# Forty extra full-height products in the first head of an attention kernel

## The reference

```
xn = layernorm(x)
q, k, v = split(xn @ w_qkv.T)          # 16 heads of 16
q, k = rope(q), rope(k)
attn = softmax(q @ k.T / 4)
x + (attn @ v) @ w_out.T + (silu(xn @ wg.T) * (xn @ wu.T)) @ wd.T
```

## Time and profile before

| | before |
|---|---|
| median of 3 runs | 2939.09 us (2939.03 to 2942.41) |
| the profiled execution | 2940.6 us |
| its span | 2938.8 us |
| mean granted PE clock | 0.989 |
| busy share of PE, DVE, ACT | 98%, 91%, 84% |

### The profile page before, as it was taken

How to read it: one execution, slowest core, us unless ns; L and a number is a source line. 1 busy time by engine, 2 the same in 40 slices (tenths; PEclk the granted TensorE clock), 3 DMA queues, 4 the chain that set the end, 5 groups by cost and what they waited for, 6 DMA issues and landing times.

```text
span 2938.8 us, 67492 instructions
## 1 busy us (share of the span) xinstructions
PE 2871.5 (98%) x27448; PEld 1062.6 (36%) x27448; DVE 2671.8 (91%) x2938; ACT 2478.5 (84%) x4635; POOL 523.0 (18%) x1086
## 2 busy tenths in 40 slices
PE   6999998999999999999999999999999999999999
PEld 4656664233333333333333333333333333333336
DVE  7667667999999999999999999999999999999952
ACT  4544554999999999999999999999999999999972
POOL 4666673000000000000000000000000000000000
PEclk9999997999999999999999999999999999999999
DMA  3233331011111111111111111111111111111125
GB/s 116 89 92 116 100 94 54 25 32 31 31 31 31 31 31 31 31 31 31 31 31 31 31 31 31 31 31 31 31 31 31 31 31 31 31 31 31 31 64 179
DMA packets 124601, 137.14 MB, mean 47 GB/s; under 512 B 43264, under 2 KB 103296, under 8 KB 124288
## 3 DMA queue, kind: packets, MB, share of 16 engines
q1 hardware_dynamic: 124288, 132.79, 16.6%
HBM read 88.15 MB, written 34.08 MB: 42 GB/s over the span
## 4 chain that ended last, share of the span: by engine, by line
PE 88%; ACT 5%; DVE 4%; issue 2%; DMA 1%; POOL 0%; SPq 0%; DVEq 0%; ACTq 0%; POOLq 0%
PE psum L749 37%; PE psum L714 21%; PE psum L785 17%; PE psum L623 5%; PE psum L594 4%; ACT probs L948 3%; PE psum L696 2%; ACT acc_sb L918 1%; DVE row_max L1355 1%; PE psum L638 1%; ACT hT L842 1%; DVE stats L1114 1%; DVE xnT L1138 1%; DVE h L1271 0%; ACT silu L855 0%
## 5 line engine op out<-in xcount | busy, mean ns | idle before, releaser
L1355 DVE TENSOR_REDUCE row_max<-psum 128x1 f32<-128x1024 f32 x2022 | 2303.0, 1211 | 27.8 <-PE psum L714 27.0
L948 ACT ACTIVATE probs<-psum 128x512 f32<-128x512 f32 x4096 | 2179.1, 595 | 164.3 <-PE psum L785 61.9
L749 PE MATMUL psum<-probs,v_op 128*32 128x256 f32 x15872 | 1297.3, 399 | 0.0
L785 PE MATMUL psum<-q_op,k_op 51*128 51x512 f16 x4096 | 854.9, 381 | 19.1 <-ACT probs L948 15.6
L714 PE MATMUL psum<-k_op,q_op 48*128 48x512 f16 x4070 | 808.2, 389 | 7.2 <-DVE row_max L1355 4.7
L714 PEld LDWEIGHTS psum<-k_op,q_op 48*128 48x128 f16 x4070 | 196.7, 93 | 855.3 <-DVE row_max L1355 537.1
L749 PEld LDWEIGHTS psum<-probs,v_op 128*32 128x32 f32 x15872 | 312.5, 108 | 524.2 <-issue 485.5
L785 PEld LDWEIGHTS psum<-q_op,k_op 51*128 51x128 f16 x4096 | 365.0, 94 | 257.4 <-ACT probs L948 68.0
L1095 POOL TENSOR_TENSOR acc_sb<-acc_sb,inv_rows 128x512 f32<-128x512 f32 x64 | 81.7, 1276 | 1686.7 <-DMA inv_rows<-inv_dram 1686.7
L623 PE MATMUL psum<-xnT,wf 128*128 128x512 f16 x768 | 179.0, 379 | 0.6 <-DVE v_space L1261 0.6
L849 ACT ACTIVATE parts<-qk_rot 128x512 f16<-128x512 f32 x64 | 40.1, 627 | 149.1 <-POOL qk_rot L1018 149.1
(11 more groups left out here) (115 smaller groups left out, 1104.1 us busy)
## 6 DMA issues: line engine op xcount, KB each, us to landing
qk_dram<-staged SPq DMA_DIRECT2D x64, 256.0 KB, 4.9
q_op<-qk_dram SPq DMA_DIRECT2D x128, 128.0 KB
k_op<-qk_dram SPq DMA_DIRECT2D x128, 128.0 KB
x_ln<-in_x SPq DMA_DIRECT2D x16, 512.0 KB, 4.4
x_res<-in_x SPq DMA_DIRECT2D x16, 512.0 KB, 5.3
y_dram<-y_blk SPq DMA_DIRECT2D x16, 512.0 KB, 3.3
k_op<-qk_dram SPq DMA_DIRECT2D x128, 64.0 KB
q_op<-qk_dram SPq DMA_DIRECT2D x128, 64.0 KB
```

The costliest lines, as they stand in the source:

```text
L749: mm = pe.matmul(bank(7)[32 * j:32 * j + 32, n0:n1], v_op[:, h % 2, t, :], probs[:, g3 % PROBS, j * BANK + n0:j * BANK + n1], start=(t == ...
L785: pe.matmul(bank(b), k_op[r:e, h % SLOTS, t * P:(t + 1) * P], q_op[r:e, h % SLOTS, j * BANK:(j + 1) * BANK], start=True, stop=True).then_i ...
L948: nc.scalar.activation(probs[:, g2 % PROBS, j * BANK:(j + 1) * BANK], bank(b), ACT.Exp, scale=to_score).then_inc(s2_used, 1)
L1355: nc.vector.tensor_reduce(row_max[:, hl % 2, t, half:half + 1], psum[:, 2 * half * BANK:(2 * half + 2) * BANK], AX.X, ALU.max).then_inc(s1 ...
```

## The change

After each `max_half` of the steps 0 to 19 PE makes one more product: the 16-bit identity (128 x 128) times 512 columns of all 128 rows of `k_op`, into bank 7. That is 40 products. Nothing reads them, and no semaphore is added or counted. Bank 7 is first needed by `weigh_v` in step 21, which overwrites it.

```diff
+        def keep_busy(c):
+
+
+            if c < FIRST2 + PV_LAG - 1:
+                pe.matmul(bank(7), identh[:, :], k_op[:, 0, 0:BANK], start=True, stop=True)
+
         def step(c):
...
             if c < N1:
                 max_half(c, 0)
+            keep_busy(c)
...
                     weigh_v(0)
                     if c < N1:
                         max_half(c, 1)
+                    keep_busy(c)
```

## The result

| | before | after |
|---|---|---|
| median of 4 runs each | 2939.61 us | 2962.97 us (2961.35 to 2963.67) |
| span of the profiled execution | 2938.8 us | 2960.7 us |
| mean granted PE clock | 0.989 | 0.986 |

The ratio of the times is 1.0081, with a 95% interval of 1.0069 to 1.0093. The forecast was 2961.4 us.

What follows compares the result with a forecast made beforehand. PE, DVE and POOL set the pace in turn within 48 us at half clock, PE in (b). Lost cover and new products 15.8 us plus switches 6.5 us gave 22.3 us on 2939.1: 2961.4 us, range 2940 to 2966.

Steps and rivals of the forecast that it cites:

- (b): Stretch from 479.8 to 503 us, 13 steps (2 to 14) at 1.2 GHz, paced by PE at 1.71 us each.
- The step of seven products: In (b), a step holds seven products one after another, 2.99 us for 1.71; 15.8 us over the stretch.
- The switch: Going between half-height and full-height products on PE loses 0.11 to 0.16 us each time, 0.13 taken.
- The term of 6.5 us: Price of 50 switches between half-height and full-height products on the path, at 0.13 us; bounds 0 and 8 us.
- The clock would not be held: Around stage B, the new products would not keep PE at full clock; forecast with clock as before, chance 0.70.
- The case that the clock never falls: Rival: full clock from `k_neg` through (b), 2934.2 to 2940.4 us; chance 0.18, including a clock back equally early.
- the 2.1 us at the products with v: DVE's waits of 0.58, 0.75 and 0.75 us for PE at the first products with v, saved if the clock is full.
- The eight products of the steps 15 to 18 and those of step 19: After (b): the eight hidden under DVE's 1.15 us; step 19 costs 0 to 0.9 us, taken as 0.
- The cover of 0.04 us: In steps 15 to 18, the time to spare for the new products under DVE's 1.15 us.
- the clock back within (b): Rival: full clock returns during the stretch, +10.8 us or 2949.9 us; chance 0.12.
- the slow 48 us: Half-rate clock from just before 475 us to 522.7 us; anything the change gives back or adds lies there.
- A lost microsecond is not won back: After the first products with v, DVE is at its own pace again, so time lost earlier stays lost.

Runs made afterwards that it cites:

- burst run: Sixteen more full-height products just before PE's wait for `k_neg`, added to the changed kernel: 2945.95 us, ratio 1.0024 to the kernel before.
- the best version: Against the kernel before: half-height products up to step 14, two full-height each half step in steps 15 to 18, three in step 19: 2934.7 us, ratio 0.9986.

## Why the prediction was right, point by point

- **The bound of (b)** was read rightly: PE's rows 64 to 111, with nothing to spare. The steps with differences lost 1.73 us each.
- **The step of seven products** (2.99 us): right, and shown part by part by the runs with one product a step (2.36 us) and with 64 columns (2.69 us).
- **The switch**: taken at 0.13 us, measured at 0.11 (0.54 and 0.53 for 0.43 us of work). The single row at 507.61 in the earlier trace rows was the right neighbour; those of the products with v were a little high. The term of 6.5 us is 50 x 0.11 = 5.5 at the measured size, and with it (b) should lose 15.8 + 5.5 = 21.3 us; it lost 21.5.
- **The clock would not be held**: so it came, but the reason was only half of it. I had set the idle 1.8 us before stage B and the missing cover in the wait for `k_neg` against two short products. The run with the first four products shows that they can carry the clock to 481 us in some executions, and then the differences lose it. What I had not seen is that the new products do hold a full clock (burst run) and only fail to restore a lost one. The case that the clock never falls was taken to gain or lose little, +1.3 us at the likelier end. The nearest run is the burst with the new products: (b) began 4.23 us later there (484.06 against 479.83), which is the burst, and of the 6.85 us between the medians 2.6 are left. The clock was lost again at 516 us in it, so the 2.1 us at the products with v were not saved as they are in the +1.3.
- **The eight products of the steps 15 to 18 and those of step 19** were taken at 0, with 0.9 as the bound. They cost 1.1 us, and a further 0.7 came from one more half step with v at the slow clock, which had been left open at 1 us either way. The cover of 0.04 us was right for the steps in which DVE had a half in hand; at step 19 there was less.
- **The rivals**: the clock back within (b) did not come in the changed kernel. It did with half-height products, of which I had expected a clock of 0.50 as before. That a clock still full at `k_neg` stays full through (b) holds with the new products and not without them. And the reason given for the small gain, that DVE and POOL bound most of the slow 48 us, was wrong: by the earlier trace rows PE set the pace in 24 us of (b) and in the 6 us with v. The gain is small since DVE and ACT take over at 1.47 us a step.
- **A lost microsecond is not won back**: true up to the last head (23.6 us), where 1.7 us came back by a shorter wait and a shorter slow stretch.
- **The total**, 22.3 us against 23.4, is closer than its parts. The switch was taken 1.0 us too high; +0.3 at the start of (b), +1.1 and +0.7 behind it were not in the sum, and the 1.7 us won back in the last head, which I had not foreseen, cancel most of them. The profiled executions lie 21.9 us apart and the medians 23.4, so a microsecond of agreement means nothing here. That part is luck; the 21.5 us of (b) are not.

What stays open is why the clock falls at 475.5 us in one execution and at 481.4 in another of the same instructions, and by which measure of PE's work it comes back. The runs order the cases; they don't give the rule.

## What to carry to other kernels

Filler work for TensorE was free here where it had the shape of what runs beside it. A product that takes all rows stops the others that share the array by halves, pays a switch each way, and can cost more than the clock that it is to save; even where three of them in each place brought the clock back, the kernel lost 10 us. Put fillers in the part of the array that is empty, or under another engine's time, and see first what the clock is worth at that place: here DVE and ACT took over at 1.47 us a step, so that the whole prize was some 5 us (3.1 there and 2.1 at the products with v), of which the best version got 4.7.

## What the runs showed of the hardware

- PE starts a half-height product beside others that stand ahead of it in the program: line 714's second product, four places behind, began 0.01 us after the first difference (487.41 and 487.42). DVE, which waits for it, started only after the last of the differences ahead of it had ended (489.37 against 489.29), so it seems to count as done in the order of the program; in the kernel before the same holds (489.44 against 489.37). The ends are modelled, so this is a reading.
- Half-height fillers brought the clock back among the differences in four traces of four (at 490.0 us in the first), where one full-height product in each place did not in 46 us, and three in each place did at 478.1 us.
- The same 25 full-height products kept the clock at 1.00 from 484 to 516 us if it was full at the start, and left it at 0.50 if it was not.
- A switch between half-height and full-height products costs 0.11 us at 1.2 GHz, even for a product of 64 columns, and as much at 2.4 GHz (in the burst run 489.10 to 489.42, 0.32 us for 0.21 us of work).
